# The causal mask of the max pieces: an add inside VectorE's maximum in place of a TensorE product

## The chip, the core and the metric

The kernel runs on one core of a Trainium2 chip. The metric is the device time of one execution in microseconds (us), median of the runs. The core has five engines that run side by side, each with its own in-order program: TensorE (PE, matrix products into PSUM), VectorE (DVE), ScalarE (ACT), GpSimd (POOL) and SyncE (SP), which here issues the DMAs. They wait for each other through semaphores.

## The reference

One transformer layer on 2048 tokens of width 512, in float32: layer norm, an attention block with 32 query heads in 8 groups (4 query heads share one key and one value head of width 64), then layer norm and a feed-forward block with ternary weights. What matters here is the attention core:

```python
q = _rope(q)
k = _rope(k)
qk = jnp.einsum('bghsd,bgxpd->bghsp', q, k) * DQK ** (-0.5)
causal = jnp.tril(jnp.ones((s, s), dtype=bool))
qk = jnp.where(causal, qk, -jnp.inf)
attn = jax.nn.softmax(qk, axis=-1)
o = jnp.einsum('bghsp,bgxpd->bghsd', attn, v)
```

The softmax needs a value near the maximum of each query's row to subtract. Only keys up to the query itself may count in it.

## The kernel before

Four stages run one after the other: `normalise`, `attention`, `output_projection`, `feed_forward`. Only `attention` is touched. It walks over the 8 groups, two to a pass of a loop on the engines (`Fori`), after a short `OPENING`. A group has 16 units; a unit is one query head (`h`, 0 to 3) and one chunk of 512 queries (`c`, 0 to 3). Unit u has 4(c+1) steps, one per tile of 128 keys, so the early units of a group are short (4 steps) and the late ones long (16).

The order of all engines is written out ahead by the table `SLOTS`: one slot per step. In each slot TensorE computes the scores of a step (`scores`, L558, L559, and L562, which adds a mask on diagonal tiles), some "pieces", sometimes a projection of the next chunk (`project`, L528, 12 matmuls), and the product with the values of the step five slots earlier (`values`, L575, L577, L579). ScalarE takes the exponential (L630). The part of it that a 16-bit number loses is computed as `pl`, three eighths of it by VectorE (L706) and five eighths by GpSimd (L784); `values` waits for it (`wait_low`).

A **piece** is what this change is about. It is one product of a 128-query tile with up to 512 keys (L541), made only to find each query's maximum. Unit u+2's pieces are computed during unit u. VectorE reduces each piece to one column of `mpart` (L714), and after the last piece of a unit it reduces `mpart` to the row maximum (L722), which a DMA transposes into `q_lm` for the scores of that unit. Each unit has 4(c+1) pieces, and 4 of them, one per query tile, reach the diagonal (`kk == c`): they are 128, 256, 384 and 512 keys wide. On those a second matmul (L544) of a scaled identity with a constant adds -30000 squared above the diagonal. Pieces and projections share four PSUM banks in turn (`SIDE = 4`): TensorE may start the r-th of them only when VectorE has read the one four before (`take_bank`, semaphores `maxs_used` and `v_low`).

A projection leaves its bank in this order: ScalarE copies the value columns (L638), then VectorE makes three instructions (L733, L734, L736), and the last frees the bank. VectorE's program is one line of work, so while it waits for ScalarE's copy, the reductions behind it wait too.

The waits that matter, in code:

```python
r = side_of(part).index(item)                       # take_bank, TensorE
if r >= SIDE:
    side_read(*side_of(part)[r - SIDE])             # waits for maxs_used or v_low
...
dve.wait_ge(maxs_ready, gg * PIECES + n + 1)        # reduce_piece, VectorE
...
pe.wait_ge(exp_done, g * STEPS + i + 1 + EXP_AHEAD) # values, TensorE
wait_low(pe, g, i)
```

## Time and profile before

| what | us |
|---|---|
| three runs | 2228.74, 2228.29, 2226.76 |
| their median | 2228.29 |
| the profiled execution, its own time | 2228.65 |
| its span in the trace | 2226.8 |
| attention, from the first to the last unit's output copy | 114.7 to 1640.1 |
| TensorE's granted clock, mean over the span | 0.974 of full speed |

The execution's own time is 1.85 us more than its span; nothing of the change lies there. A busy engine in a view is one with an instruction in flight; TensorE's are pipelined, so its busy share says that work was queued, and not that it ran at its peak rate. Three stretches of attention, taken together, are one full group in the steady state: 1002.2 to 1073.8 (the long units at the end of the fifth group and the hand-over to the sixth), 1073.8 to 1123.4 (the short units at the start of the sixth) and 1123.4 to 1190.1 (its middle). They are called the **late**, the **early** and the **middle** stretch.

### The profile page before, as it was taken

How to read it: one execution, taken by the hardware profiler on the slowest of the kernel's cores; microseconds unless marked ns; L12 is line 12 of the kernel's file. 1: busy time of each engine (PE TensorE's matmuls, PEld its weight loads, DVE VectorE, ACT ScalarE, POOL GpSimd, SP SyncE). 2: the span in 40 equal slices, each digit the busy share in tenths (PEclk: the TensorE clock that was granted, in tenths of full speed). 3: DMA queues.
4: the chain of work that ended last, by engine and by line, in shares of the span. 5: the costliest groups of instructions: out<-in, count | busy, mean ns of one | idle time of the engine just before them, and what ended most of it. 6: DMA issues, size and time to landing. Idle time of an engine off the chain costs nothing. (4 is left out here: it accounts for less than half of the span.)

```text
span 2226.8 us, 61948 instructions
## 1 busy us (share of the span) xinstructions
PE 2040.7 (92%) x22271; PEld 1257.0 (56%) x22271; DVE 1578.4 (71%) x2975; ACT 994.8 (45%) x2216; POOL 1256.0 (56%) x1340
## 2 busy tenths in 40 slices
PE   1599999989999998999999899989989888999998
PEld 1356666656666665566666566666654444444443
DVE  8479879958977995897799589789856664222221
ACT  3245555554565554456455455645553331211210
POOL 5456776766777676677667676866742331311311
PEclk7799999999999999999999999999999999999999
DMA  5421132222213112211311221132145541000000
GB/s 173 135 47 35 30 67 46 35 44 51 35 33 79 36 31 48 52 33 30 80 35 35 50 45 35 35 74 38 33 111 195 165 130 29 1 19 19 0 19 19
DMA packets 227728, 123.00 MB, mean 55 GB/s; under 512 B 186080, under 2 KB 207328, under 8 KB 225888
## 3 DMA queue, kind: packets, MB, share of 16 engines
q1 hardware_dynamic: 227424, 119.00, 22.6%
q8 instruction: 184, 3.01, 0.6%
q14 instruction: 120, 0.98, 0.2%
HBM read 50.53 MB, written 25.17 MB: 34 GB/s over the span
## 5 line engine op out<-in xcount | busy, mean ns | idle before, releaser
L784 POOL TENSOR_TENSOR pl<-p 128x512 f16<-128x512 f32 (+3 forms) x801 | 764.9, 969 | 208.7 <-ACT p L630 195.1
L630 ACT ACTIVATE p<-a_ps 128x512 f32<-128x512 f32 (+3 forms) x1283 | 662.9, 533 | 379.5 <-PE a_ps L559 198.1
L714 DVE TENSOR_REDUCE mpart<-a_ps 128x1 f32<-128x512 f32 (+3 forms) x1288 | 722.4, 599 | 141.3 <-PE a_ps L544 71.1
L575 PE MATMUL a_ps<-v,p 128*128 128x65 f16 x4352 | 529.4, 193 | 22.6 <-DVE pl L706 15.1
L577 PE MATMUL a_ps<-v,p 128*128 128x64 f16 x4352 | 530.4, 194 | 0.0
L579 PE MATMUL a_ps<-v,pl 128*128 128x65 f16 x4352 | 527.0, 192 | 0.0
L575 PEld LDWEIGHTS a_ps<-v,p 128*128 128x128 bf16 x4352 | 410.4, 97 | 142.2 <-DVE pl L706 33.7
L541 PE MATMUL a_ps<-k_hl,q_hh 128*128 128x512 f16 (+3 forms) x1288 | 444.1, 349 | 50.6 <-issue 18.5
L558 PE MATMUL a_ps<-q_hh,k_hl 128*128 128x512 f16 (+3 forms) x1283 | 446.6, 348 | 18.8 <-DMA q_lm<-qk_lo 18.8
L706 DVE TENSOR_TENSOR pl<-p 128x512 f16<-128x512 f32 (+2 forms) x482 | 440.5, 917 | 19.6 <-ACT p L630 19.6
L577 PEld LDWEIGHTS a_ps<-v,p 128*128 128x128 bf16 x4352 | 407.0, 98 | 83.3 <-issue 0.6
L559 PE MATMUL a_ps<-q_lm,k_h 128*128 128x512 f16 (+3 forms) x1283 | 447.0, 348 | 0.0
L579 PEld LDWEIGHTS a_ps<-v,pl 128*128 128x128 f16 x4352 | 407.9, 99 | 0.0
L541 PEld LDWEIGHTS a_ps<-k_hl,q_hh 128*128 128x128 f16 x1288 | 125.7, 98 | 162.8 <-issue 29.6
L808 POOL TENSOR_TENSOR onorm<-osb,rden 128x256 f32<-128x256 f32 x128 | 78.5, 614 | 240.7 <-DVE rden L741 234.5
L1278 POOL TENSOR_TENSOR f_hl<-f_hid,f_hh 128x512 f16<-128x512 f32 x64 | 74.2, 1162 | 239.7 <-DVE f_hh L1248 239.7
L1193 PE MATMUL f_ps<-xh,tern 128*128 (+1 forms) x512 | 195.0, 381 | 1.8 <-DVE f_credit L1235 1.8
L1193 PE MATMUL f_ps<-xl,tern 128*128 (+1 forms) x512 | 194.8, 380 | 0.0
L528 PE MATMUL a_ps<-wh,yh 128*128 128x384 f16 x544 | 180.3, 331 | 7.1 <-DVE wl L698 6.2
L528 PE MATMUL a_ps<-wl,yh 128*128 128x384 f16 x544 | 180.2, 331 | 0.0
L528 PE MATMUL a_ps<-wh,yl 128*128 128x384 f16 x544 | 179.8, 331 | 0.0
L1229 ACT ACTIVATE f_silu<-f_ps,tern_scale 128x512 f32<-128x512 f32 x64 | 44.0, 688 | 256.2 <-PE f_ps L1193 256.2
(100 smaller groups left out, 2849.9 us busy)
## 6 DMA issues: line engine op xcount, KB each, us to landing
attn_scratch<-onorm SPq DMA_DIRECT2D x32, 512.0 KB, 3.4
p_att<-attn_scratch SPq DMA_DIRECT2D x64, 256.0 KB, 3.3
raw<-ffn_t SPq DMA_DIRECT2D x12, 1024.0 KB, 6.3
wraw<-w_in_t SPq DMA_DIRECT2D x9, 768.0 KB, 6.0
resid_scratch<-xin SPq DMA_DIRECT2D x4, 1024.0 KB, 4.3
raw<-w_out_t SPq DMA_DIRECT2D x1, 4096.0 KB, 15.2
x<-resid_scratch SPq DMA_DIRECT2D x4, 1024.0 KB, 6.7
out<-x SPq DMA_DIRECT2D x16, 256.0 KB, 2.0
```

The costliest lines, as they stand in the source:

```text
L528: last = nc.tensor.matmul(bank[:, 0:GC], a[:, kt, tok], b[:, kt, :], start=(kt == 0 and n == 0), stop=(kt == KT - 1 and n == 2))
L541: last = nc.tensor.matmul(bank[:, 0:width], q_hh[:, c % 2, h, t * P:(t + 1) * P], k_hl[:, par ^ ahead, kk * CHUNK:kk * CHUNK + width], sta ...
L558: nc.tensor.matmul(out, k_hl[:, side, keys], q_hh[:, c % 2, h, r * P:CHUNK], start=True, stop=False)
L559: last = nc.tensor.matmul(out, k_h1[:, side, keys], q_lm[:, c % 2, h, r * P:CHUNK], start=False, stop=not diag)
L575: nc.tensor.matmul(o, weights, v[:, par, j, 0:VU], start=(j == 0 and t == 0), stop=False, skip_group_check=True)
L577: nc.tensor.matmul(o[:, 0:DH], weights, v[:, par, j, VL:VW], start=False, stop=False, skip_group_check=True)
L579: last = nc.tensor.matmul(o, pl[:, i % RING, t * P:(t + 1) * P], v[:, par, j, 0:VU], start=False, stop=(j == TPC * c + t), skip_group_chec ...
L630: nc.scalar.activation(p32[:, i % RING, r * P:CHUNK], sbank(i)[:, r * P:CHUNK], ACT.Exp, scale=SCALE).then_inc(exp_done, 1)
L706: nc.vector.tensor_tensor(pl[:, i % RING, cols], p32[:, i % RING, cols], p_high[:, i % RING, cols], ALU.subtract).then_inc(low_dve, 1)
L714: nc.vector.reduce_max(mpart[:, u % 2, t, kk:kk + 1], side_bank(part, ("piece", ahead, u, i))[:, 0:width], AX.X)\
L784: nc.gpsimd.tensor_tensor(pl[:, i % RING, cols], p32[:, i % RING, cols], p_high[:, i % RING, cols], ALU.subtract).then_inc(low_pool, 1)
L1193: last = nc.tensor.matmul(bank, w[:, k, e * P:(e + 1) * P], x[:, k, bass.ds(c * CHUNK, CHUNK)], start=(k == 0 and x is xh), stop=(k == KT ...
```

## The change

The mask matmul of the diagonal pieces (L544) goes. VectorE gets a constant `causal` in SBUF, 512 columns of float32: zeros, and in the last 128 columns 0 on and below the diagonal and -3e37 above it. On a diagonal piece its reduction is no longer `reduce_max` but one `tensor_tensor_reduce`: it adds `causal` to the piece, writes the sum as bfloat16 into a buffer `masked` that nobody reads, and keeps the maximum. Ahead of it stands a one-column `memset`, which carries the waits. Other pieces stay as they were. The mask of the scores themselves (L562) stays on TensorE.

```diff
+LEAST = 3e37
...
+        causal = sb("causal", [P, CHUNK], F32)
+        masked = sb("masked", [P, 2, CHUNK], BF16)
...
-                    last = nc.tensor.matmul(bank[:, 0:width], q_hh[:, c % 2, h, t * P:(t + 1) * P],
-                                            k_hl[:, par ^ ahead, kk * CHUNK:kk * CHUNK + width], start=True, stop=(kk < c))
-                    if kk == c:
-                        last = nc.tensor.matmul(bank[:, width - P:width], big, mask_qk, start=False, stop=True)
-                    last.then_inc(maxs_ready, 1)
+                    nc.tensor.matmul(bank[:, 0:width], q_hh[:, c % 2, h, t * P:(t + 1) * P],
+                                     k_hl[:, par ^ ahead, kk * CHUNK:kk * CHUNK + width], start=True, stop=True)\
+                        .then_inc(maxs_ready, 1)
...
+            nc.vector.memset(causal[:, 0:CHUNK - P], 0.0)
+            nc.vector.tensor_scalar(causal[:, CHUNK - P:CHUNK], mask_qk, LEAST / 3e4, None, ALU.mult).then_inc(causal_set, 1)
+            dve.wait_ge(causal_set, 1)
...
-                    nc.vector.reduce_max(mpart[:, u % 2, t, kk:kk + 1], side_bank(part, ("piece", ahead, u, i))[:, 0:width], AX.X)\
-                        .then_inc(maxs_used, 1)
+                    bank = side_bank(part, ("piece", ahead, u, i))[:, 0:width]
+                    if kk < c:
+                        nc.vector.reduce_max(mpart[:, u % 2, t, kk:kk + 1], bank, AX.X).then_inc(maxs_used, 1)
+                    else:
+                        if ahead or n >= 2:
+                            dve.wait_ge(maxs_used, gg * PIECES + n - 1)
+                        nc.vector.memset(credit[:, 13 + n % 2:14 + n % 2], 0.0)
+                        nc.vector.tensor_tensor_reduce(masked[:, n % 2, 0:width], bank, causal[:, CHUNK - width:CHUNK], 1.0, -LEAST,
+                                                       ALU.add, ALU.max, mpart[:, u % 2, t, kk:kk + 1]).then_inc(maxs_used, 1)
```

VectorE's program in the middle of a group, between two of the four instructions that split the next group's weights (`wl`, L698 before, L703 after), before:

```order
L698 SCALAR_TENSOR_TENSOR wl<-wraw,wh 128x384 [waits w_high]
L706 TENSOR_TENSOR pl<-p 128x512 [waits exp_done]
L713 REGISTER_ALU
L714 TENSOR_REDUCE mpart<-a_ps 128x1 [waits maxs_ready]
L741 RECIPROCAL rden<-osb 128x4 [waits o_out]
L713 REGISTER_ALU
L714 TENSOR_REDUCE mpart<-a_ps 128x1 [waits maxs_ready]
L713 REGISTER_ALU
L714 TENSOR_REDUCE mpart<-a_ps 128x1 [waits maxs_ready]
```

And the same place in the changed kernel:

```order
L703 SCALAR_TENSOR_TENSOR wl<-wraw,wh 128x384 [waits w_high]
L711 TENSOR_TENSOR pl<-p 128x512 [waits exp_done]
L718 REGISTER_ALU
L721 TENSOR_REDUCE mpart<-a_ps 128x1 [waits maxs_ready]
L753 RECIPROCAL rden<-osb 128x4 [waits o_out]
L718 REGISTER_ALU
L725 MEMSET credit 128x1 [waits maxs_used,maxs_ready]
L726 ISA masked,mpart<-a_ps,causal 128x256
L726 ISA mpart 128x1
L718 REGISTER_ALU
L721 TENSOR_REDUCE mpart<-a_ps 128x1 [waits maxs_ready]
```

The first of the two reductions behind the reciprocal was that of a diagonal piece of 256 keys. One instruction has become three in the same place: the memset, the add-and-max, and a read that brings the maximum out of the engine into `mpart`. Nothing else moved.

TensorE's program a little further on, at a diagonal piece of 384 keys, before:

```order
L558 MATMUL a_ps<-q_hh,k_hl 128x512
L559 MATMUL a_ps<-q_lm,k_h 128x512
L562 MATMUL a_ps<-consts 128x128
L507 REGISTER_ALU
L541 MATMUL a_ps<-k_hl,q_hh 128x384
L544 MATMUL a_ps<-consts 128x128
L428 REGISTER_ALU
L575 MATMUL a_ps<-v,p 128x65
```

And in the changed kernel:

```order
L560 MATMUL a_ps<-q_hh,k_hl 128x512
L561 MATMUL a_ps<-q_lm,k_h 128x512
L564 MATMUL a_ps<-consts 128x128
L511 REGISTER_ALU
L545 MATMUL a_ps<-k_hl,q_hh 128x384
L432 REGISTER_ALU
L577 MATMUL a_ps<-v,p 128x65
```

Only the mask matmul behind the piece is gone; the scores' own mask matmul (L562, now L564) is still there.

VectorE's program at the start of attention, where its credits release the other engines, in the changed kernel:

```order
L692 MEMSET v 128x32
L693 MEMSET causal 128x384
L694 TENSOR_SCALAR causal<-consts 128x128
L698 MEMSET credit 128x1 [waits causal_set]
L698 MEMSET credit 128x1 x6
L699 MEMSET credit 128x1
```

Before, the memset of `v` was followed at once by the seven credits and the last one, which is the second count that ScalarE, TensorE and GpSimd wait for.

## Rows read from the trace of the kernel before

**Rows 1.** The page's first part: busy time, share, instructions of each engine

```profile
PE 2040.7 (92%) x22271; PEld 1257.0 (56%) x22271; DVE 1578.4 (71%) x2975; ACT 994.8 (45%) x2216; POOL 1256.0 (56%) x1340
```

**Rows 2.** Windows: stretch, us; busy PE, PEld, DVE, ACT, POOL (instructions); clock, DMA

```profile
1002.20:1073.80 71.60, 69.16 (x1016) 47.33 (x1015) 53.74 (x99) 42.31 (x94) 55.64 (x59) 1.00 0.25 50
1073.80:1123.40 49.60, 46.48 (x561) 30.44 (x560) 41.90 (x91) 24.21 (x63) 31.74 (x39) 1.00 0.27 58
1123.40:1190.10 66.70, 64.83 (x861) 42.32 (x859) 64.05 (x118) 38.08 (x89) 46.28 (x52) 1.00 0.19 33
```

**Rows 3.** Waits in the middle stretch: us in total, times, longest

```profile
PEld a_ps L575 <- DVE pl L706: 3.4, 5, 1.5
...
DVE rope_a L733 <- ACT v L638: 1.7, 3, 0.9
DVE mpart L714 <- PE a_ps L541: 0.7, 2, 0.6
```

**Rows 4.** Waits in the early stretch

```profile
PEld a_ps L541 <- DVE v L736: 2.7, 3, 1.4
PEld a_ps L541 <- DVE mpart L714: 1.6, 1, 1.6
...
DVE mpart L714 <- PE a_ps L541: 2.9, 3, 1.4
DVE rope_a L733 <- ACT v L638: 2.5, 3, 1.1
```

**Rows 5.** Waits in the late stretch

```profile
PE a_ps L558 <- DMA q_lm<-qk_lo: 1.7, 2, 1.2
...
DVE rope_a L733 <- ACT v L638: 8.5, 5, 2.7
```

**Rows 6.** Windows of the mask matmul (L544) alone: busy PE and PEld (instructions)

```profile
1002.20:1073.80 71.60, 4.98 (x23) 2.25 (x23) 1.00 0.25 50
1073.80:1123.40 49.60, 4.82 (x22) 2.15 (x22) 1.00 0.27 58
1123.40:1190.10 66.70, 4.16 (x19) 1.86 (x19) 1.00 0.19 33
```

**Rows 7.** Timeline of TensorE at a diagonal piece: start, us, instruction

```profile
1150.77 0.22 PE L544 MATMUL a_ps<-consts 128*128 128x128 f16 x1
1150.82 0.19 PE L575 MATMUL a_ps<-v,p 128*128 128x65 f16 x1
```

**Rows 8.** Groups of VectorE by form, 60 to 1680 us: busy, mean ns, idle before

```profile
L714 DVE TENSOR_REDUCE mpart<-a_ps 128x1 f32<-128x512 f32 x898 | 586.7, 680 | 81.4 <-PE a_ps L541 46.8 <-PE a_ps L544 30.1
...
L733 DVE TENSOR_TENSOR rope_a<-a_ps,cos_sb 128x320 f32<-128x320 f32 x136 | 66.5, 489 | 114.9 <-ACT v L638 114.9
...
L1051 DVE TENSOR_TENSOR p_atl<-p_ps,p_ath 128x512 f16<-128x512 f32 x12 | 8.1, 687 | 10.6 <-ACT p_ath L1011 10.6
```

**Rows 9.** Timeline, start of attention and of output projection: memsets

```profile
65.10 0.12 DVE L693 MEMSET credit<- 128x1 f32 x7
...
65.41 1.76 ACT L621 ACTIVATE wh<-wraw 128x384 f16<-128x384 f32 x4 [2.90 <-DVE credit L694]
...
1667.67 0.69 DVE L1070 BATCH_NORM_STATS2 p_stats<-x 128x6 f32 x1
1667.70 0.06 DVE L1069 MEMSET p_credit<- 128x1 f32 x1
```

**Rows 10.** Timeline of ScalarE in the normalise stage: an accumulator read

```profile
10.24 0.19 ACT L191 ACTIVATION_READ_ACCUMULATOR n_sq<-n_ln 128x1 f32 x1
10.34 0.61 ACT L191 ACTIVATE n_sq<-n_ln 128x512 f32<-128x512 f32 x1
```

**Rows 11.** Timeline of VectorE in the middle stretch: a short instruction and the next

```profile
1149.19 0.16 DVE L741 RECIPROCAL rden<-osb 128x4 f32<-128x4 f32 x1
1149.28 0.99 DVE L714 TENSOR_REDUCE mpart<-a_ps 128x1 f32<-128x256 f32 x2
```

**Rows 12.** Source view of a 128-column memset: min, median, max ns

```profile
L1044 DVE MEMSET p_ones<- x1: 165/165/165, 1645.6 to 1645.6; 128x128 f32 x1
```

More of the change, by code:

```diff
@@ L396, in attention @@
         ones_set = sem("ones_set")
+        causal_set = sem("causal_set")
         rows_set = sem("rows_set")
```

## The prediction

> **What bounds the kernel now.** I read the engine totals first: TensorE is busy for 92% of the span, VectorE for 71% [rows 1]. That invites the conclusion that taking matmuls away pays and that VectorE has room. It is an average over four stages, and the change lies only in attention, so next I cut one full group of attention into three stretches and read the busy times there [rows 2]. Now VectorE looks different: in the middle stretch it is busy for 64.05 of 66.7 us (96%), in the early one for 41.90 of 49.6 (84%), in the late one for 53.74 of 71.6 (75%). TensorE is busy for 97%, 94% and 97%. Then the waits, to see who holds whom. In the middle TensorE's weight loads wait 3.4 us for VectorE's `pl` (L706), and VectorE itself waits only 2.4 us in all [rows 3]: there VectorE is the engine that sets the pace at least part of the time. In the early stretch both wait for each other: TensorE 2.7 us for the instruction that frees a projection's bank and 1.6 us for a reduction, VectorE 2.9 us for pieces and 2.5 us for ScalarE's copy of a projection [rows 4]. In the late stretch VectorE stands 17.9 us idle (71.6 less 53.74 [rows 2]), 8.5 of them in front of L733, and TensorE waits for a transposed `q_lm` (1.7 us) and for little else [rows 5]: TensorE sets the pace. TensorE's clock is 1.00 in all three, its upper level of 2.4 GHz, so a TensorE term is worth the same everywhere.
>
> **What is removed.** Each diagonal piece loses one matmul of 128 columns. Its row says 0.22 us, but the matmuls overlap: the next one starts 0.05 us after it (1150.77 to 1150.82) [rows 7]. 128 columns at 2.4 GHz are 0.053 us, and with the small gap between instructions I take 0.057. A group has 23 + 22 + 19 = 64 of them in the three stretches [rows 6], and there are 520 with the opening's eight: 520 x 0.057 = **29.6 us** if TensorE were the bound at every one. That is the most that the change can give.
>
> **What is added.** On VectorE one reduction becomes three instructions, and I cost them by the time until the next instruction can start, not by their own rows, since VectorE's instructions overlap too. (a) The add-and-max. The trace has none, so I bound it by the nearest rows. A plain reduction of 512 columns out of PSUM takes 680 ns; a `tensor_tensor` of 512 columns with one operand in PSUM and one in SBUF takes 687 (L1051), and one of 320 columns takes 489 while GpSimd works beside it (L733) [rows 8]. So a second operand from SBUF costs about +10 ns, and nothing in these rows speaks for a collision with GpSimd. Below that end is nothing; above it, an operation that took two cycles per column would add some 330 ns at the mean width of 320 columns; no row with one PSUM operand does that, so I keep it only as a rival. (b) The memset. Seven of them take 0.12 us together and a single one 0.06, which leaves 10 ns each; one stands beside the instruction it precedes as if it cost nothing [rows 9]. I take 10, with 0 and 60 as its ends. (c) The read of the maximum. VectorE has no such row. ScalarE's accumulator read lasts 0.19 us, and the next instruction starts 0.10 us after it (10.24 to 10.34) [rows 10]. VectorE's own shortest instruction with an input, the reciprocal of four columns, occupies 0.09 us (1149.19 to 1149.28) [rows 11]; one without an input, a memset, 0.01. The read has no input from memory but must wait for the last maximum, so it lies nearer the upper rows: I take 70 ns, with 10 and 186 (no overlap at all) as ends. The sum is **+90 ns** for each diagonal piece, with ends 20 and 255. Over 520 it is 47 us of VectorE's time, more than TensorE saves. The new wait on `maxs_used` is for the reduction two pieces back on the same engine. That one has ended before the piece in front of it began, so the wait costs nothing; behind the memset stand only this piece's own instructions.
>
> Against (b) and (c) speaks a rule. The Trainium skill ("VectorE: DVE Perf Modes", sections "Side-by-side: where the cycles go for N=2048 bf16" and "The DRAIN you can't avoid") gives every VectorE instruction about 150 cycles of fixed cost and says that the next does not start until the pipe is empty; its advice is to keep the number of instructions small. Two instructions more would be an estimated 2 x 157 = 314 ns by that page, not 80. The trace disagrees: the reciprocal's 0.16 us leaves 0.09 until the next start [rows 11], and seven memsets fit in 0.12 us [rows 9]. I go by the rows and keep the rule's outcome as the second rival, priced below from rows.
>
> (d) Once, at the start of attention: a memset of 384 columns and a scaling of 128 ahead of the credits, and a wait for it. A 128-column memset takes 165 ns [rows 12] and a one-column one 60 [rows 9], so 384 columns take about 0.38 us; with the scaling and the wait some 0.7 us. ScalarE waits there for the last credit (2.90 us) [rows 9], so this is on the path: **+0.7 us**.
>
> **What of it lies on the path.** Stretch by stretch:
>
> - *Middle, 19 diagonal pieces.* VectorE's work becomes 64.05 + 19 x 0.09 = 65.8 us in 66.7. Of its 2.65 us idle, 1.7 are in front of L733, where it waits for ScalarE's copy of what TensorE has just projected [rows 3]; those waits follow TensorE and take up extra work only if it stands right before them. I count 11 pieces in front of one of TensorE's waits for VectorE (+0.09 each), and 7 to 8 where TensorE leads (-0.057 each): +1.0 - 0.4 = **+0.6**.
> - *Early, 22 pieces.* VectorE has 7.7 us idle, and the instruction for which TensorE waits (L736) stands right behind an L733 that itself waited for TensorE's projection through ScalarE [rows 4]. So time goes by TensorE's pace in part: full would be 22 x 0.057 = -1.25; I take half, **-0.6**, since the reductions behind those waits come late by the same 0.09 and one of them holds TensorE for 1.6 us.
> - *Late, 23 pieces.* VectorE has 17.9 us idle, the added 2.1 fit in it, and TensorE's 23 x 0.057 = -1.3 counts but for the waits for a DMA [rows 5]: **-1.1**.
>
> A group gives -1.1 us, eight give -9; with (d) and a little for the opening the sum is **-8 us**. The profiled execution took 2228.65, which is 0.36 above the median of the runs, so I forecast 2221 (-0.33%). If VectorE's idle time were no cover at all (the late stretch as full as the middle one), the same edit would cost 64 x 0.09 = 5.8 us per group and 46 in all.
>
> **The rivals.** About 0.2% (4.5 us) is what can be told from no change.
>
> 1. *The balance closes: no change.* At about 160 ns per piece the middle stretch needs 64.05 + 19 x 0.16 = 67.1 us, more than it has now, and with some of the 1.7 us before L733 still in it grows by about 1.3; the early one gives 0.2 and the late one 1.1: zero, 2224 to 2233. For it: VectorE's 96%. Against it: it needs a read of 140 ns of occupancy, above every row. Some error in my count of pieces that TensorE waits for would do it too. 0.22.
> 2. *Slower: VectorE's queue becomes the bound of the first 116 us of each group.* One mechanism: the add-and-max and its read do not overlap their neighbours. With the ends of rows 9 and 10 (60, 186 and 10, so 256 ns) the middle needs 64.05 + 4.86 = 68.9 and keeps about 1 us of idle time: +3.2; the early one needs 41.9 + 5.6 = 47.5 and 2.5 us of waits before L733, plus what it cannot fill: +1.2; the late one gives -0.8. That is +3.6 per group, +29, so 2258. It decides from about 180 ns per piece on (above +4.5 us). For it: the place is real, TensorE already waits there for L706. Against it: rows 9 and 11 show overlap for every kind of short instruction. 0.27 for slower in all, 0.12 for above 2243. The skill's rule on fixed costs, named above, would end in this case; worked out like the others from rows, two instructions with the full 0.16 us of the reciprocal's row are 320 ns: middle +4.4, early +2.0, late -0.7, together +46 and 2275.
> 3. *All of TensorE's time comes back.* If the read costs 10 ns like a memset, the pieces come ready 0.057 us earlier and cost VectorE 0.03 more, the middle turns to about -0.5 and the early to -1.2: -3 per group, 2204. 0.05.
>
> The forecast's own case, 2206 to 2224, has 0.46.
>
> **How the numbers follow.** The forecast's time is 2221. Faster by over 0.2%: 0.46 + 0.05 = 0.51; within it 0.22; slower 0.27. The range of 8 in 10 leaves 0.06 below and 0.12 above: 2206 to 2243. The forecast's own range is 2206 to 2224.
>
> **What the profile after would show.** Right: no matmul on the mask behind the pieces, 520 add-and-max instructions with means within 15 ns of the reductions of the same width, and reads after which the next instruction starts within 0.1 us; the late stretch shorter by about 1.1 us, the middle longer by about 0.6, TensorE's waits for `pl` in it longer than 3.4 us, VectorE's busy share there about 98%. Wrong: an add-and-max whose mean is well above 680 ns at 512 columns, or a start-to-start of read plus memset above 0.15 us; then the early and the middle stretch both grow. The prediction also fails if the late stretch does not shrink: then something other than TensorE's columns, the transposes or the hand-over between groups, sets its length.

## The result, and the profile after

The changed kernel takes 2231.59 us (median of 20 runs, 2223.91 to 2239.09), the kernel before in the same rounds 2228.34 (20 runs, 2223.42 to 2231.58). The ratio is 1.0018, 95% interval 1.0011 to 1.0026: slower by 0.11% to 0.26% (+3.3 us by the medians), where 2221 had been forecast. The profiled execution of the change took 2232.03 us, its span is 2230.2.

TensorE lost what it was to lose, 520 matmuls, and VectorE got its 1042 instructions (the page's first part and its instruction queues; q8 holds pieces of TensorE's code, as the fills below show, q14 those of other engines; packets, MB, share of the DMA engines):

```profile
PE 2019.8 (91%) x21751; PEld 1227.1 (55%) x21751; DVE 1594.0 (71%) x4017; ACT 994.9 (45%) x2216; POOL 1251.2 (56%) x1340
...
q8 instruction: 180, 2.95, 0.5%
q14 instruction: 133, 1.09, 0.2%
```

TensorE's busy time fell by 20.9 us, VectorE's rose by 15.6 [rows 1]. VectorE's groups by form, 60 to 1680 us (count, busy, mean ns, idle before):

```profile
L721 DVE TENSOR_REDUCE mpart<-a_ps 128x1 f32<-128x512 f32 x768 | 503.0, 680 | 50.8 <-PE a_ps L545 48.0
L726 DVE CUSTOM_DVE_ANT_0 masked<-a_ps,causal 128x512 bf16<-128x512 f32 x130 | 88.7, 682 | 27.0 <-issue 19.8 <-DVE mpart L721 6.5
L726 DVE CUSTOM_DVE_ANT_0 masked<-a_ps,causal 128x384 bf16<-128x384 f32 x130 | 71.4, 549 | 9.1 <-issue 9.1
...
L726 DVE DVE_READ_ACCUMULATOR2_ANT mpart<- 128x1 f32 x520 | 41.5, 80 | 0.0
...
L725 DVE MEMSET credit<- 128x1 f32 x520 | 30.7, 59 | 23.2 <-issue 18.6 <-PE a_ps L545 4.5
```

The add-and-max of 512 columns takes 682 ns, the plain maximum 680. Around it, in order of time (VectorE, start and us):

```profile
1151.96 0.68 DVE L721 TENSOR_REDUCE mpart<-a_ps 128x1 f32<-128x512 f32 x1
1152.57 0.55 DVE L726 CUSTOM_DVE_ANT_0 masked<-a_ps,causal 128x384 bf16<-128x384 f32 x1
1152.59 0.06 DVE L725 MEMSET credit<- 128x1 f32 x1
1153.05 0.08 DVE L726 DVE_READ_ACCUMULATOR2_ANT mpart<- 128x1 f32 x1
1153.05 0.68 DVE L711 TENSOR_TENSOR pl<-p 128x512 f16<-128x512 f32 x1
```

The next instruction (L711) starts with the read, at 1153.05, so read and memset take nothing from the queue. From the start of an add-and-max to the start of what follows, it is 13 to 26 ns more than behind a plain maximum of the same width (198, 331 and 464 ns for 128, 256 and 384 columns before), some 20 ns. Only where a masked piece of 128 columns is followed at once by another masked one, in 17 places, it is about 100 ns more.

TensorE's wait for `pl` in the middle stretch, 3.4 us before [rows 3], is longer, as was forecast:

```profile
PEld a_ps L577 <- DVE pl L711: 4.7, 9, 1.5
```

The three stretches of the same group, as windows (columns as in [rows 2]):

```profile
1001.60:1072.70 71.10, 67.90 (x993) 46.08 (x992) 53.53 (x147) 42.31 (x93) 55.53 (x59) 1.00 0.23 50
1072.70:1122.50 49.80, 45.48 (x539) 29.23 (x538) 42.85 (x133) 24.24 (x63) 31.69 (x39) 1.00 0.28 58
1122.50:1189.00 66.50, 64.17 (x841) 40.98 (x839) 64.72 (x155) 38.08 (x89) 45.82 (x52) 1.00 0.15 32
```

Late 71.6 → 71.1, early 49.6 → 49.8, middle 66.7 → 66.5 us [rows 2]. Two are shorter; the early one is not.

**Cutting attention finer.** Each group copies the output of its 16 units out of the bank in turn (ScalarE, `osb`). I call the time from the copy of unit u to that of u + 1 interval u. Thirteen of the sixteen repeat to 0.01 or 0.02 us from one even group to the next and from one odd group to the next, and between kernels that differ only in fillers, but for a rare 0.1 to 0.3 in intervals 1 and 10 (intervals 1, 2 and 7 are some 0.1 us apart between even and odd groups). Three do not: interval 4, where TensorE waits for the transposed keys of the third chunk, and 15 and 0, the hand-over to the next group, where it waits for `q_lm` transposes and where, after every second group, each engine's loop branches back. Changed kernel less kernel before, by the starts of these copies:

| part | us |
|---|---|
| opening, to the first copy (114.66 → 116.26) | +1.6 |
| the 13 intervals that repeat, 8 groups | -9.4 |
| interval 4, 8 groups | +4.1 |
| intervals 15 and 0 | +6.8 |
| to the last copy (1640.12 → 1643.19) | +3.1 |

So the gain that was forecast is there, -9.4 us or -1.17 per group. Something outside the forecast's sum takes it back in three intervals and the opening. The experiments look for it.

### The profile page after: what moved, and what is told of

Read it like the earlier page. It is cut to its first block and busy times, and to the rows that moved or that the text cites. A ratio compares the mean times of both kernels' runs of the same rounds, so it can differ in the third digit from the quotient of the medians.

```text
span 2230.2 us, 62469 instructions
## 1 busy us (share of the span) xinstructions
PE 2019.8 (91%) x21751; PEld 1227.1 (55%) x21751; DVE 1594.0 (71%) x4017; ACT 994.9 (45%) x2216; POOL 1251.2 (56%) x1340
## 3 DMA queue, kind: packets, MB, share of 16 engines
q8 instruction: 180, 2.95, 0.5%
## 5 line engine op out<-in xcount | busy, mean ns | idle before, releaser
L577 PE MATMUL a_ps<-v,p 128*128 128x65 f16 x4352 | 530.6, 193 | 29.6 <-DVE pl L711 21.1
L721 DVE TENSOR_REDUCE mpart<-a_ps 128x1 f32<-128x512 f32 x768 | 503.0, 680 | 50.8 <-PE a_ps L545 48.0
L711 DVE TENSOR_TENSOR pl<-p 128x512 f16<-128x512 f32 (+2 forms) x482 | 442.2, 920 | 18.9 <-ACT p L632 18.9
L726 DVE CUSTOM_DVE_ANT_0 masked<-a_ps,causal 128x128 bf16<-128x128 f32 (+3 forms) x520 | 248.8, 483 | 68.2 <-issue 60.2
## 6 DMA issues: line engine op xcount, KB each, us to landing
raw<-w_out_t SPq DMA_DIRECT2D x1, 4096.0 KB, 14.6
```

The lines of the kernel that those rows point to most:

```text
L577: nc.tensor.matmul(o, weights, v[:, par, j, 0:VU], start=(j == 0 and t == 0), stop=False, skip_group_check=True)
L711: nc.vector.tensor_tensor(pl[:, i % RING, cols], p32[:, i % RING, cols], p_high[:, i % RING, cols], ALU.subtract).then_inc(low_dve, 1)
L721: nc.vector.reduce_max(mpart[:, u % 2, t, kk:kk + 1], bank, AX.X).then_inc(maxs_used, 1)
```

## The experiments

All times are medians of runs taken beside the kernel before (2227.85, 2227.7, 2226.32 and 2228.4 us in the four sets); the brackets are the 95% interval of the ratio to it. The five right columns, in us, are worked out from each one's profile, less that of the kernel before, as in the table above (its last row is the last column here). A profile is one execution, up to 5.3 us away from its run's median (e1's 2226.76 against 2232.09, e2's 2213.50 against 2218.54). The thirteen intervals do not show this scatter; the columns beside them may hold a few us of it.

| run | median us | ratio | opening | 13 | 4 | 15+0 | last |
|---|---|---|---|---|---|---|---|
| the change | 2231.59 | 1.0018 (1.0011-1.0026) | +1.6 | -9.4 | +4.1 | +6.8 | +3.1 |
| e1_setup_late | 2232.09 | 1.0017 (1.0007-1.0026) | +0.6 | -9.6 | +4.1 | +2.5 | -2.3 |
| e2_pe_half_only | 2218.54 | 0.9963 (0.9951-0.9975) | -2.6 | -11.6 | +3.7 | -4.7 | -15.3 |
| e3_dve_half_only | 2242.51 | 1.0062 (1.0049-1.0075) | +1.1 | +1.1 | +1.0 | +8.9 | +12.1 |
| e4_narrow_mask | 2235.74 | 1.0028 (1.0017-1.0039) | +2.3 | -4.3 | +1.1 | +9.9 | +9.0 |
| g1_after_fill16 | 2228.70 | 1.0001 (0.9990-1.0013) | +1.3 | -9.4 | +4.8 | +3.4 | 0.0 |
| g2_before_fill25 | 2236.30 | 1.0035 (1.0022-1.0049) | +2.4 | -0.3 | +0.6 | +4.3 | +7.1 |
| g3_fill16_pe51 | 2238.16 | 1.0040 (1.0027-1.0054) | +3.2 | -9.4 | +11.5 | +0.5 | +5.8 |
| g4_before_fill40 | 2244.98 | 1.0071 (1.0057-1.0085) | +2.2 | 0.0 | +13.7 | +1.5 | +17.4 |
| h1_after_place | 2215.33 | 0.9954 (0.9939-0.9969) | +2.5 | -9.1 | -1.3 | -6.0 | -13.9 |
| h2_after_place_late | 2217.67 | 0.9960 (0.9946-0.9974) | +2.0 | -9.4 | -1.5 | -5.7 | -14.6 |
| h3_before_place | 2235.35 | 1.0041 (1.0026-1.0056) | +0.7 | +0.1 | +9.6 | -5.9 | +4.4 |
| h4_after_pe150 | 2222.32 | 0.9985 (0.9975-0.9994) | +4.4 | -9.6 | -2.3 | -2.9 | -10.4 |
| i1_before_pe100 | 2236.51 | 1.0033 (1.0020-1.0046) | -0.3 | -0.2 | +5.1 | +0.6 | +5.2 |
| i2_before_pe150 | 2239.82 | 1.0047 (1.0031-1.0063) | +2.2 | -0.1 | +3.3 | +5.9 | +11.3 |
| i3_before_pe200 | 2230.86 | 1.0012 (1.0003-1.0021) | +7.0 | -0.2 | +2.3 | -10.5 | -1.4 |
| i4_after_pe200 | 2220.57 | 0.9967 (0.9956-0.9978) | +8.9 | -9.1 | -1.4 | -8.3 | -10.0 |

### The two halves apart

**e1_setup_late**: the change with its three set-up lines (`causal`) moved behind the last credit.

```diff
-            nc.vector.memset(causal[:, 0:CHUNK - P], 0.0)
-            nc.vector.tensor_scalar(causal[:, CHUNK - P:CHUNK], mask_qk, LEAST / 3e4, None, ALU.mult).then_inc(causal_set, 1)
-            dve.wait_ge(causal_set, 1)
...
             nc.vector.memset(credit[:, 15:16], 0.0).then_inc(ones_set, 1)
+            nc.vector.memset(causal[:, 0:CHUNK - P], 0.0)
+            nc.vector.tensor_scalar(causal[:, CHUNK - P:CHUNK], mask_qk, LEAST / 3e4, None, ALU.mult).then_inc(causal_set, 1)
+            dve.wait_ge(causal_set, 1)
```

> The changed kernel, with the set-up of the causal constant moved behind the credits that release the other engines. Theory A (TensorE's saving is real in the stretches that it paces, but is given back at the waits for transposed keys and queries, which land later because TensorE's own instruction fetches now fall into them, plus 1.5 us of set-up): about 1.5 us faster than the changed kernel, so some 2230 where the kernel before has 2228.3, ratio 1.001; the late waits at the keys (about 2.2 us against 1.3 before) stay. Rival B (VectorE's added work costs what TensorE saves): also 1.5 us, and the same waits. Rival C (the set-up is all of it): the whole gain of some 8 us comes back, 2222.

2232.09: no gain that can be measured. In the change the set-up takes longer than forecast (timeline of VectorE):

```profile
64.67 0.38 DVE L693 MEMSET causal<- 128x384 f32 x1
64.97 1.31 DVE L694 TENSOR_SCALAR causal<-consts 128x128 f32<-128x128 f16 x1
66.42 0.23 DVE L698 MEMSET credit<- 128x1 f32 x7
```

ScalarE's wait for the last credit, 2.90 us before [rows 9], is 4.73 us in the change and again 2.90 with the late set-up, and the opening does come 1.0 us earlier in the profile of this run. It is a minor term.

**e2_pe_half_only**: the kernel before without the mask matmul; VectorE as before, so the maxima leave out the causal mask.

```diff
-                                            k_hl[:, par ^ ahead, kk * CHUNK:kk * CHUNK + width], start=True, stop=(kk < c))
-                    if kk == c:
-                        last = nc.tensor.matmul(bank[:, width - P:width], big, mask_qk, start=False, stop=True)
+                                            k_hl[:, par ^ ahead, kk * CHUNK:kk * CHUNK + width], start=True, stop=True)
```

> The kernel before without the mask matmul of the pieces; VectorE as before, no set-up. It leaves the mask out of the maxima (they run over later keys of the diagonal block too). TensorE's instructions are exactly those of the changed kernel. Theory A: TensorE's fetches fall as in the changed kernel, so the key transposes of the third chunk land about 4.5 us after their issue, as there; the time is the changed kernel's less the set-up (1.5) and less 20 ns for each piece in VectorE's tight stretches (about 3): 2226 to 2228. Rival B: VectorE's addition was the whole loss, so here the full TensorE saving shows: 2199 to 2206.

**e3_dve_half_only**: the change with the mask matmul kept behind each diagonal piece (the mask is added twice).

```diff
+                    if kk == c:
+                        last = nc.tensor.matmul(bank[:, width - P:width], big, mask_qk, start=False, stop=True)
```

> The changed kernel with the mask matmul kept on TensorE, so that the mask is added twice. TensorE's instructions are exactly those of the kernel before, VectorE's those of the changed one. Theory A: keys land as in the kernel before (the last at 3.8 to 4.3 us after the issue), VectorE's addition of about 20 ns a piece costs 2 to 5 us, the set-up 1.5: 2231 to 2235. Rival B: VectorE's addition costs as much as TensorE saved, some 20 us or more: 2250.

**e4_narrow_mask**: as e3, but the kept matmul is one column wide and adds zeros, so TensorE's instructions are as many as before.

```diff
+                        last = nc.tensor.matmul(bank[:, width - P:width - P + 1], big, mask_qk[:, 0:1], start=False, stop=True)
```

> The changed kernel with the mask matmul kept as a product of a single column that adds zeros: as many TensorE instructions at the same places as in the kernel before, but only about half of the matmul's time. Theory A: the fetches fall as in the kernel before, the keys land as there, TensorE saves about 25 to 30 ns of 57 for each piece; with the set-up 2222 to 2227, so faster than the changed kernel although TensorE does more. Rival B: TensorE's extra 27 ns for 520 pieces is lost where TensorE sets the pace, 2235 or more.

In the thirteen steady intervals TensorE's half is worth -11.6 us and VectorE's +1.1, which is 2 ns per piece. With TensorE's half already in, VectorE's costs 2.2 us there (from -11.6 in e2 to -9.4 in the change), 4 ns per piece. VectorE's three instructions are not what makes the change slow: the second rival falls, and so does my +90 ns. Yet as whole kernels the halves are worth -9.3 and +14.7 us; e2 came between the two ranges written down for it, and so did e3. 8.9 us of e3's loss stand in intervals 15 and 0, and most of these are not waits. TensorE is busy there for 7.1 us more with the same matmuls, at a lower granted clock. The interval 15 of the first pass end in e3, and under it in the kernel before:

```profile
487.94:503.77 15.83, 9.18 (x67) 5.73 (x68) 5.86 (x30) 2.41 (x7) 3.68 (x6) 0.61 0.37 86
486.94:500.57 13.63, 7.27 (x67) 4.71 (x68) 5.34 (x14) 2.30 (x8) 3.68 (x6) 0.75 0.42 94
```

In the change TensorE is busy for 1.8 us less in intervals 15 and 0 than before, and idle for 8.6 us more: there it is waits.

e4 was expected at 2222 to 2227 and came at 2235.74. That is the figure of its rival (2235 or more), but not for the rival's reason, since the thirteen intervals give 4.3 us back. Its interval 4 did what was hoped (+1.1 instead of +4.1 with TensorE's old instruction count), but the hand-over is the worst of all. The hand-overs are of two kinds, three at the end of a pass of the loop and four inside one (less the kernel before, each with the interval 0 behind it; the very first interval 0 stands by itself, at -0.1 to -1.4 us):

| run | three at pass ends | four inside a pass |
|---|---|---|
| the change | +3.0 | +4.7 |
| e2 (TensorE's new program, VectorE's old) | -9.0 | +5.2 |
| e3 (VectorE's new program, TensorE's old) | +9.2 | -0.1 |
| e4 (as e3, one column) | +11.8 | -0.4 |

So three things were to be explained: interval 4 and the hand-overs inside a pass, which in these four runs go with TensorE's instruction count, and the pass ends, where VectorE's new program costs 9 to 12 us and TensorE's gives 6 to 9 back.

### Where the code lies

At a back-branch VectorE stops for 4 to 7 us in every kernel. In the change a second stop follows (VectorE, second pass end):

```profile
877.75 0.06 DVE L725 MEMSET credit<- 128x1 f32 x1 [5.72 <-issue]
877.79 0.29 DVE L726 CUSTOM_DVE_ANT_0 masked<-a_ps,causal 128x128 bf16<-128x128 f32 x1
878.01 0.08 DVE L726 DVE_READ_ACCUMULATOR2_ANT mpart<- 128x1 f32 x1
878.08 0.06 DVE L725 MEMSET credit<- 128x1 f32 x1
878.12 0.42 DVE L726 CUSTOM_DVE_ANT_0 masked<-a_ps,causal 128x256 bf16<-128x256 f32 x1
878.47 0.08 DVE L726 DVE_READ_ACCUMULATOR2_ANT mpart<- 128x1 f32 x1
880.10 0.06 DVE L725 MEMSET credit<- 128x1 f32 x1 [1.56 <-PE a_ps L545]
```

The profile puts the 1.56 us down to a TensorE piece. But the same stop stands behind the same, twelfth, instruction of the loop (register and wait instructions counted) at all three pass ends of the change, of e1, e3 and e4, 1.35 to 1.95 us each, and never in the kernel before. Its place in VectorE's program is the 196th instruction. The change has 25 more instructions ahead of its loop (three for set-up, the rest the longer pieces of the opening), so its loop begins at the 184th and not the 159th. Hence the experiment: fillers that do nothing, to shift the code.

**g1_after_fill16**, **g2_before_fill25**, **g4_before_fill40** (VectorE; one instruction holds two waits), **g3_fill16_pe51** (as g1, and on TensorE ahead of its opening):

```diff
             nc.vector.memset(credit[:, 15:16], 0.0).then_inc(ones_set, 1)
+            for _ in range(32):          # g2: 50, g4: 80
+                dve.wait_ge(ones_set, 2)
...
+            for _ in range(102):         # g3 only
+                pe.wait_ge(ones_set, 2)
             group(0, 0, OPENING)
             with pe.Fori(0, GROUPS // 2) as pair:
```

> The changed kernel with 16 more instructions on VectorE ahead of its loop over pairs of groups (waits that hold already, two to an instruction). Nothing of the work is changed. Theory P (where the code lies): in every profile with VectorE's new program (the change, the late set-up, VectorE's half alone, the one-column mask) VectorE stops for 1.35 to 1.9 us behind the twelfth instruction after each back-branch of its loop, at its 196th instruction, which would be where the next 8 KB piece of its code (128 instructions) begins; the kernel before, whose loop begins 25 instructions earlier, has no such stop. Moved on by 16, the loop begins behind that border and the stop is gone: 3 back-branches x 1.4 us, and the half-clock stretches that follow: 4 to 6 us off the change, 2226 (2224 to 2229), and the profile has no idle time at VectorE's 13th instruction behind the branch. Theory W (the work itself: three instructions per piece where TensorE waits for VectorE after the branch): no change, 2231 to 2233, and the stop is still there.

> The kernel before with 25 more instructions on VectorE ahead of its loop (waits that hold already), so that its loop begins at the 184th instruction, as in the changed kernel, 12 ahead of the supposed border. Theory P: VectorE stops for about 1.4 us behind its twelfth instruction after each of the 3 back-branches, and the kernel is 3 to 6 us slower than before: 2231 to 2234. Theory W: no difference beyond the fillers' own time in the opening, under 1 us: 2228 to 2229.

> The changed kernel with the 16 fillers on VectorE and 51 more instructions on TensorE ahead of its opening group (waits that hold already). In the change, the 16 KB pieces of TensorE's code are fetched 2.1 to 2.3 us behind the issue of the keys' transposes in every group, whose landing is then 4.5 to 4.7 us after the issue against 3.8 to 4.4, and TensorE waits 2.2 us for the third chunk's keys against 1.3 (interval 4: +0.5 to +0.6 us a group); 51 instructions are a fifth of such a piece, some 2.4 us, so that the fetches fall at the issue. Theory F (the fetch sets the landing): interval 4 comes down to about +0.1, some 4 us less than the run with VectorE's fillers alone, 2222 (2219 to 2226). Without it: as that run, within 1 us.

> The control: the kernel before with 40 more instructions on VectorE ahead of its loop, which begins at the 199th instruction, 3 behind the supposed border and 125 ahead of the next. More filler than the run with 25. Theory P: no stop behind the branch, 2227 to 2229. If filler as such costs (the opening, or any shift of VectorE's code), it is slower than the run with 25 fillers.

g1 came at 2228.70, 2.9 us under the change (the kernel before stood at 2227.7 beside the one and 2228.34 beside the other), and the stop is gone at all three pass ends:

```profile
881.60 0.06 DVE L727 MEMSET credit<- 128x1 f32 x1
881.64 0.42 DVE L728 CUSTOM_DVE_ANT_0 masked<-a_ps,causal 128x256 bf16<-128x256 f32 x1
881.99 0.08 DVE L728 DVE_READ_ACCUMULATOR2_ANT mpart<- 128x1 f32 x1
882.00 0.55 DVE L728 CUSTOM_DVE_ANT_0 masked<-a_ps,causal 128x384 bf16<-128x384 f32 x1
```

g2 brought the stop into the kernel before, behind the twelfth instruction, at all three pass ends, but only for 0.38, 0.19 and 0.50 us. The first:

```profile
497.75 0.29 DVE L716 TENSOR_REDUCE mpart<-a_ps 128x1 f32<-128x128 f32 x1
498.42 0.42 DVE L716 TENSOR_REDUCE mpart<-a_ps 128x1 f32<-128x256 f32 x1 [0.38 <-issue]
```

The sizes agree all the same. VectorE resumes its loop (with a register instruction) at 495.81 here and at 877.52 in the change, and goes on past the border at 498.42 and 880.10: 2.6 us later in both, and 2.4 to 2.7 us at all six pass ends of the two. The stop lasts for as much of this time as the instructions ahead of the border do not fill: six maxima in the kernel before, two masked pieces in the change. So this stop is shown, and that the place of the code makes it. In g1's profile the three pass ends are 4.9 us shorter than in the change's; by the medians, each against the kernel before beside it, g1 is some 2 us faster.

But g2 (+8.6 us, where 3 to 6 had been expected) and g4 (+17, where theory P expected nothing, and has no stop at the branch indeed) are far slower than that. g4's loss stands in interval 4: +2.7 to +3.0 us in the even groups, +0.5 to +0.7 in the odd ones. g3's too, +1.8 to +3.3 in the odd groups; it was a miss, 2238.16 where 2222 had been expected. Moving code moves something else.

### What is fetched while the keys are under way

Traffic from the issue of the third chunk's keys on, 4.5 us in group 5. First the change: pieces of code (q8, q14) and the transposes with their time to landing, then the window of interval 4:

```profile
q8 instruction: 1, 0.02, 1.4%
q14 instruction: 1, 0.01, 0.7%
...
k_hl<-qk_lo SPq DMA_TRANSPOSE x1, 3.4
```

```profile
1100.64:1110.25 9.61, 7.60 (x110) 5.01 (x109) 8.07 (x22) 4.31 (x10) 6.87 (x9) 1.00 0.52 113
```

g3, where three pieces fall into the same 4.5 us, two of q14 and one of q8:

```profile
q14 instruction: 2, 0.02, 5.5%
q8 instruction: 1, 0.02, 2.0%
...
k_hl<-qk_lo SPq DMA_TRANSPOSE x1, 4.6
```

```profile
1106.38:1117.17 10.79, 7.60 (x110) 4.96 (x109) 8.07 (x22) 4.31 (x10) 6.87 (x9) 1.00 0.76 100
```

TensorE's and VectorE's work is the same to 0.05 us, 7.60 and 8.07, and the interval is 1.18 us longer: that is the landing of `k_hl` (3.4 → 4.6). In this window the kernel before has a piece of q14 but none of q8, `k_hl` lands after 2.6 us, and the interval is 8.87:

```profile
q14 instruction: 1, 0.01, 0.5%
...
k_hl<-qk_lo SPq DMA_TRANSPOSE x1, 2.6
```

```profile
1102.11:1110.98 8.87, 7.77 (x114) 5.20 (x113) 8.05 (x15) 4.31 (x10) 6.87 (x9) 1.00 0.59 121
```

Over the eight groups of each profile, from the issue of the first transpose (`k_h`) to the landing of both:

| fetches under way | both landed after |
|---|---|
| none of TensorE's, at most one of another engine's (before, odd groups; i1, i2, i4, h1, even groups) | 3.7 to 4.0 us |
| none of TensorE's, two of other engines' at 2.1 to 2.6 (h1, i4, odd groups; g4, odd groups) | 4.0 to 4.2; 4.4 to 4.5 |
| TensorE's 0.3 to 0.4 us ahead of the issue (before, even groups) | 4.0 to 4.4 |
| TensorE's 0.2 to 1.8 ahead, another engine's at 2.2 to 2.9 (i2, odd groups) | 4.5 to 4.6 |
| TensorE's 2.0 to 2.3 us behind it (the change; h3, odd groups) | 4.5 to 4.7 |
| TensorE's between 0.2 ahead and 1.9 behind, one or two of other engines' at 2.1 to 3.3 (g3 and i1, odd groups) | 5.0 to 5.8 |

TensorE's wait for the keys follows this one for one (0.9 to 3.2 us). In eleven of these intervals over all runs, with waits of 2.0 to 2.9 us, the clock fell as well. g4's interval 4 of group 4 has a wait of 2.7 us and this window:

```profile
923.12:935.30 12.18, 9.45 (x114) 6.01 (x112) 8.23 (x16) 4.31 (x10) 6.86 (x9) 0.86 0.36 84
```

The kernel before needs 9.20 us for it with the clock at 1.00; here the mean granted clock is 0.86, TensorE's two levels mixed, and its busy time is 1.6 us more for the same 114 matmuls. Not each long wait did this (g3's of 3.2 us in group 5, above, kept 1.00). What the lower clock costs by itself stands in h3, described below, in groups 1 and 3: the same 114 matmuls, the keys landed after 4.72 and 4.74 us, TensorE's wait 1.96 and 1.99 us:

```profile
332.33:343.71 11.38, 9.42 (x114) 5.89 (x113) 8.23 (x15) 4.31 (x10) 6.86 (x9) 0.85 0.44 92
720.07:729.82 9.75, 7.76 (x114) 5.19 (x113) 8.03 (x15) 4.31 (x9) 6.85 (x9) 1.00 0.50 107
```

It is 1.6 us. The clock fell so in four of g4's interval 4, in three of h3's, in two of g3's, in one each of i1's and i2's, and in none of the kernel before or of the change. About half of the +13.7 and +9.6 us that the table has for g4 and h3 is this, and a good quarter of g3's +11.5 (estimates, 1.6 us for each).

The Trainium skill ("Runtime: NRT & Kernel Launch", section "Instruction fetch mechanics") says that each engine's sequencer fetches its code by DMA in 16 KiB blocks of 256 instructions, that crossing a block is mostly hidden, and that a taken branch forces a fetch first when its target lies outside the two blocks that the engine holds. The trace agrees on the branch (stops of 4 to 7 us) and on TensorE (180 pieces, 2.95 MB: 16 KB each). The other engines' pieces are 8 KB here. And "mostly hidden" leaves out what costs most here: the engine does not stop, but the transposes in flight land later.

**h1_after_place**, **h2_after_place_late** (h1 with e1's late set-up), **h4_after_pe150** (h1 without VectorE's lines), **h3_before_place** (before, TensorE 40). The fillers stand at the kernel's start, where both engines wait for data:

```diff
             nc.vector.memset(mhalf[:, :], -0.5).then_inc(half_set, 1)
+            for _ in range(32):
+                dve.wait_ge(half_set, 1)
...
             pe.wait_ge(ident_in, 16)
+            for _ in range(300):         # h3: 80
+                pe.wait_ge(ident_in, 16)
```

> The changed kernel with its code moved and its work untouched: 16 more instructions on VectorE and 150 more on TensorE at the kernel's very start, where both wait for data (waits that hold already). The runs so far say that the intervals between the copies of two units' outputs are alike to 0.01 us in all groups and all kernels of one kind, but for three of them: interval 4 (the third chunk's keys) and intervals 15 and 0 (the hand-over to the next group), where TensorE waits for transposes; and that a landing is later by 0.7 to 1 us for each piece of code that is fetched while it is under way (third chunk's keys: 3.8 us from issue with none of TensorE's, 4.6 with one, 5.4 to 5.8 with one of VectorE's as well). In the change TensorE's fetch stands about 96 instructions behind the first instruction of a window of 100 in even groups, at the window's end in odd ones. Theory F (fetches in flight): 150 instructions ahead put it some 100 behind the window, interval 4 is that of the kernel before or less (about -0.6 to -0.8 us a group against the run with 16 fillers), 5 to 7 us off 2228.7: 2222 (2218 to 2225), which is faster than the kernel before. Theory N (position means nothing here, the gain is spent elsewhere): 2228 to 2229.

> The same with the additive mask set up behind the credits that ScalarE waits for. The opening was 0.6 us behind the kernel before with the late set-up and 1.6 with the early one. Expected: 0 to 1 us less than the run before this one, 2221 (2217 to 2225).

> The kernel before with 40 more instructions on TensorE at the kernel's start. In its even groups TensorE's fetch falls 0.3 to 0.4 us ahead of the third chunk's keys and they land after 4.0 to 4.4 us, in its odd groups far from them and they land after 3.8. 40 instructions ahead it is clear in both. Theory F: interval 4 of the even groups comes to that of the odd ones, -0.3 to -0.6 us in four groups, 1 to 3 us off: 2226 (2224 to 2228). If the kernel before was as well placed as it can be, no change. The run against the changed kernel in its place gives the change itself without the position of its code; by the intervals that repeat, the change should then be worth 1.2 to 1.4 us a group, some 10 us in all, less the opening: 4 to 8 us.

> The changed kernel with the 150 instructions on TensorE alone, VectorE's code where the change has it. Theory F with P: interval 4 as in the run with both, and the stop of 1.4 us behind VectorE's twelfth instruction at the three ends of a pass stays: 2 to 4 us over that run, 2225 (2221 to 2228).

h1 takes 2215.33, 16 us under the change and 11 under the kernel before (which stood 2 us lower beside h1 than beside the change), without a change of its work. TensorE's fetch is out of the way: it now falls 5.4 to 7.1 us behind the issue. The window of group 5 (from the issue of the keys, then interval 4) shows what is left:

```profile
q14 instruction: 2, 0.02, 1.1%
...
k_hl<-qk_lo SPq DMA_TRANSPOSE x1, 2.9
```

```profile
1091.62:1100.77 9.15, 7.59 (x110) 5.00 (x109) 8.06 (x22) 4.31 (x10) 6.86 (x9) 1.00 0.54 118
```

It gained more than the 5 to 7 us expected, since the hand-over shrank as well (15+0: -6.0 instead of +3.4 in g1). h4 shows the two effects apart: interval 4 as in h1 and the stop behind the twelfth instruction still there (1.34 to 1.42 us), 7.0 us slower than h1 where 2 to 4 was expected. Not all of the 7.0 is the stop: of the 5.6 us between the two profiles 3.1 stand in intervals 15 and 0, 1.9 in the opening and 2.1 behind attention, less 1.5 elsewhere. h2 says again that the set-up's place cannot be measured. h3 was a miss, +9.0 where -1 to -3 was expected. The odd groups' fetch moved further than I had counted, from 5.4 to 5.8 us behind the issue to 2.3, into the flight, and the landing came to 4.7 us. In the even groups 2 and 4 the keys' issue itself came 0.6 us later. And in three of its eight groups the clock fell, some 1.6 us each. Where a fetch will fall I could not compute to the microsecond; the landing once it falls there was as expected, the clock was not in the account.

### Is it the change or the place?

**i1**, **i2**, **i3**: before, TensorE filler at the start, 100, 150, 200. **i4**: as h1, with 200.

```diff
             pe.wait_ge(ident_in, 16)
+            for _ in range(200):         # i2: 300, i3 and i4: 400
+                pe.wait_ge(ident_in, 16)
```

> The kernel before with 100 more instructions on TensorE at the kernel's start (waits that hold already), work untouched. The question of this call: the changed kernel gained 13 us by the position of its code; is 2226 to 2228 the kernel before at a good position, or would it gain as much? Theory L (before stands well by luck, since in its odd groups none of TensorE's fetches falls on the third chunk's keys and in its even groups only just ahead of them): no position gives it more than about 0.4 us in each of four groups and a little in the hand-overs, so none of these three is under 2222, and some are 3 to 10 us over 2228. Theory G (any kernel gains some 10 us at the right place, and the change itself is worth nothing): one of the three is at 2215 to 2220. For this one: even groups' fetch clear of the keys, odd groups' at their issue: 2225 to 2230.

> The same with 150, the filler of the changed kernel at 2215. Even groups' fetch at the end of the keys' flight, odd groups' clear: by theory L 2228 to 2234; by theory G 2215 to 2220 here or in one of the other two.

> The same with 200. Even groups' fetch inside the keys' flight (+0.6 to +0.9 us in each of four, more where TensorE's clock falls behind it), odd groups' clear: by theory L 2229 to 2236.

> The changed kernel with 16 fillers on VectorE and 200 instead of 150 on TensorE, all at the start: is 2215 one lucky place or a broad one? The fetch comes some 50 instructions earlier, ahead of where it was by 5.4 to 6.8 us behind the issue of the keys, while TensorE waits for them or just before. If it falls behind 3.8 us: interval 4 as in the run with 150, 2214 to 2219. If it falls inside the flight: as the run with 16 fillers alone, 2222 to 2229.

None of the three reached 2222: 2236.51, 2239.82, 2230.86; the first two lie above the ranges given for them (to 2230 and 2234), the third inside its own. i4 came at 2220.57, between its two ranges, with interval 4 as in h1 and an opening 8.9 us longer. By the medians, the kernel before stood at 2228 to 2245 in seven positions (mean 2236.0), the changed kernel with its early set-up at 2215 to 2238 in six (mean 2226.1). As shipped, the first is the best of its seven and the second the fifth of its six. Theory L's totals hold, not all of its reasons: it gave the hand-over "a little", and i3's is 10.5 us shorter in the profile, hidden behind an opening 7.0 us longer (200 fillers delay TensorE's first transpose from 16.5 to 28.8 us). Taking the opening out, the best of the kernel before is 1517.1 us from first to last copy (i3) and the best of the change 1506.6 (i4): 10.5 us apart, and the means over all positions, e1 and h2 with them, 12.6. The thirteen steady intervals say 9.4. The means of the medians, openings included, are 9.9 apart. These positions are no random sample, and no two of the kernels stand at like places in all engines, so only the 9.4 is free of the place; the other readings agree with it: the change itself is worth about 10 us.

## Why the prediction was wrong

- **What bounds the kernel**: right. Where TensorE paces, an interval lost 0.056 us for each of its mask matmuls (7, 11, 12) or 0.042 (5, 9, 13); where VectorE paces (intervals 6, 8, 10) it grew by 0.05 to 0.10 us. Interval 14 grew by 0.11 too, and in e2 by the same, with VectorE's program as before; that is not explained.
- **What is removed**: right in kind, 29.6 us as the ceiling. 388 of the 520 matmuls stand in the thirteen steady intervals, 22.1 us at 0.057; e2 gave back 11.6 of them.
- **What is added, +90 ns**: mis-sized. It is about 20 ns from start to start, the lower end of the bounds, and the read that I put at 70 costs the queue nothing. The add-and-max is within 8 ns of the reductions of the same width at all four widths (forecast 15). In the steady intervals VectorE's whole half came to +1.1 us (e3), or +2.2 on top of TensorE's (the change less e2).
- **(d) the set-up, +0.7**: more than two times too small. ScalarE's wait grew by 1.8 us and the opening by 1.6; the scaling alone, which I had priced by a memset, takes 1.31. Moving it gained nothing measurable.
- **The stretches**: late -1.1 forecast, -0.5 measured; middle +0.6 forecast, -0.2 measured; early -0.6 forecast, +0.2 measured, and without interval 4 it is -0.6. My -9 for eight groups is -9.4 in the thirteen intervals, but the agreement is partly luck, since two errors cancel: too dear a piece in the middle, too large a gain in the late stretch.
- **The step that failed**: "A group gives -1.1 us, eight give -9; with (d) and a little for the opening the sum is -8 us". It takes the waits for DMAs and the hand-over as given, and so puts their change at nothing, without a reason: the edit acts only through the work that it adds and removes. It also changes the number of instructions, and so where the code is fetched. That is +4.1 us in interval 4 (shown: g3, g4, h1 and h3 move it by code position alone) and +6.8 in 15 and 0 (+3.0 at the pass ends, +4.7 inside a pass, -1.0 in the first interval 0). That position decides the latter too is shown: with 150 fillers on TensorE and the same work, h4 has -2.9 there and h1 -6.0. How it does so is shown only for the stop behind the branch. The forecast's 2221 lies within what the changed kernel takes over its places, 2215 to 2238; a hit there would have been luck.
- **The rivals**: the first, balance closed at 160 ns a piece, fell on the right time for a wrong reason. The second fell (e3), and with it the outcome that I had drawn from the Trainium skill ("VectorE: DVE Perf Modes", section "The DRAIN you can't avoid"): that the next instruction waits for the pipe to empty. The same section adds that an instruction that is not held starts earlier, and the trace agrees with that: the next one starts with the read. The third had the price nearly right (30 ns forecast, some 20 measured), but not the size: only about half of TensorE's time comes back. In the thirteen intervals of the change TensorE is busy for 17.5 us less and idle for 8.2 us more.
- **My own signs**: the rise of the wait for `pl` (3.4 → 4.7 us) and VectorE's share in the middle (97%, 98 forecast) came as said, though the middle did not grow. The sign for failure was that the late stretch does not shrink. It shrank, and the prediction failed all the same.

What stays open: the hand-over. Its 15+0 moved between -10.5 and +9.9 us over these kernels. It holds `q_lm` transposes with fetches beside them, three loads of weights at the pass ends, and the branch. In the change, between groups 2 and 3, a piece of q8 fell beside a `q_lm` transpose and TensorE waited 2.57 us there; that this is the mechanism in every case was only argued. How much of the hand-overs is TensorE's lower clock (7.1 us in e3) and how much is scatter between executions is open as well, since each kernel has one profile. g2's three losses of about 2.3 us, each at a hand-over inside a pass, are not taken apart.

## What to carry to other kernels

An edit that adds or removes instructions moves all code behind it, and with loops and transfers that an engine waits for this can cost or give more than the edit: here 9.4 us of gain against 10.9 us in the three intervals that position decides. Before judging a change of under 1%, run it and its rival with a few idle instructions ahead of the loop, and read the intervals in which nothing waits for a transfer; they repeat to 0.01 or 0.02 us and say what the edit itself is worth. And after a back-branch, see how many instructions stand ahead of the first stop that no other engine explains.

## What the runs showed that I had not expected

- A piece of TensorE's code (16 KB) fetched while two transposes are under way made them land 0.7 to 0.9 us later, with one or two of other engines' (8 KB) beside it 1.2 to 2.0. Behind such a wait TensorE's clock fell in some groups, for another 1.6 us.
- After a back-branch VectorE stopped for 4 to 7 us, three times in each kernel, and where the loop's first instruction stood 12 instructions ahead of a border, once more until 2.4 to 2.7 us after it had resumed.
- Fillers without work moved the same kernel between 2228 and 2245 us, and the changed one between 2215 and 2238.
- VectorE's add-and-max with one operand in PSUM costs 2 to 8 ns more than the plain maximum, and its accumulator read (80 ns) none of the queue.
